# Vision-transformer front end with routed experts on one core: the image held on 96 partitions, its channel sums in two products, and the second norm in a tile of its own

## The reference, cut to what matters

```python
pooled = x.reshape(64, 12, 14, 16, 14, 16).sum(axis=(3, 5))   # image: sums over 16x16 patches
h = einsum('bcij,ce->bije', pooled, channel_weights)          # 196 tokens of 192 channels
h = concatenate([h.reshape(64, 196, 192), txt], axis=1)       # + 32 text tokens = 228
h = h + attention(layernorm(h))      # 12 heads of 16, causal, a sink per head, rotary q and k
xf = layernorm(h)                    # second norm: router logits, and the rows for the experts
h = h + experts(xf)                  # top 2 of 8, capacity, 192 -> 512 gated -> 192
```

## Time and profile before

| | before |
|---|---|
| median of three runs | 2927.87 us |
| the profiled execution's own time | 2924.14 us |
| its span, first to last instruction | 2922.3 us |
| PE busy | 2783.5 us (95%) |
| DVE busy | 2029.5 us (69%) |
| ACT busy | 1692.1 us (58%) |
| POOL busy | 2019.7 us (69%) |
| mean granted PE clock | 0.979 |
| moved by DMA | 292.47 MB |

### The profile page before, as it was taken

How to read it: one execution, slowest core, us unless ns; L and a number is a source line. 1 busy time by engine, 2 the same in 40 slices (tenths; PEclk the granted TensorE clock), 3 DMA queues, 4 the chain that set the end, 5 groups by cost and what they waited for, 6 DMA issues and landing times. The chain is left out here.

```text
span 2922.3 us, 65980 instructions
## 1 busy us (share of the span) xinstructions
PE 2783.5 (95%) x21712; PEld 2512.5 (86%) x21712; DVE 2029.5 (69%) x5657; ACT 1692.1 (58%) x4074; POOL 2019.7 (69%) x2070
## 2 busy tenths in 40 slices
PE   2899999999999999999999977999999999999998
PEld 1788888888888888888888866999999989999997
DVE  3577777777777777777777745767676767676766
ACT  0466666666666666666666644656565656565655
POOL 3578888888888888888888743656565655565665
PEclk8899999999999999999999978999999999999999
DMA  6455544444444444444344223333333333323242
GB/s 187 146 178 176 172 166 170 156 122 123 120 112 108 111 122 122 123 120 115 107 109 121 57 50 64 52 61 51 64 55 63 50 65 50 66 46 66 46 69 43
DMA packets 206006, 292.47 MB, mean 100 GB/s; under 512 B 95670, under 2 KB 167675, under 8 KB 205874
## 3 DMA queue, kind: packets, MB, share of 16 engines
q1 hardware_dynamic: 82642, 241.41, 28.1%
q0 software_dynamic: 122880, 47.00, 11.5%
q10 hardware_dynamic: 352, 2.41, 0.3%
HBM read 201.73 MB, written 93.90 MB: 101 GB/s over the span
## 5 line engine op out<-in xcount | busy, mean ns | idle before, releaser
L1494 POOL DMA_INDIRECT out<-arena,who x320 | 595.3, 1860 | 290.6 <-DVE who L1373 179.4
L572 DVE TENSOR_REDUCE top<-bank 114x2 f32<-114x456 f32 (+1 forms) x576 | 352.7, 622 | 85.9 <-PE bank L931 69.5
L687 POOL TENSOR_TENSOR arena<-arena 112x896 f32<-112x896 f32 x192 | 403.2, 2101 | 12.7 <-DMA arena<-in_x 12.7
L1467 PE MATMUL bank<-w_dn,hid 128*114 128x192 f32 x3840 | 401.9, 264 | 0.0
L1467 PEld LDWEIGHTS bank<-w_dn,hid 128*114 128x114 f32 x3840 | 390.3, 180 | 0.0
L1440 ACT ACTIVATE arena<-bank 128x456 f32<-128x456 f32 x320 | 176.2, 551 | 340.9 <-PE bank L1431 330.9
L1285 POOL DMA_INDIRECT moe_rows<-row,slot x256 | 293.8, 1148 | 102.8 <-issue 84.2
L549 ACT ACTIVATE pieces<-bank 64x456 fp32r<-64x456 f32 x384 | 209.2, 545 | 134.2 <-PE bank L907 131.9
L727 POOL TENSOR_TENSOR qk<-rot_c,qk 114x384 fp32r<-114x384 f32 x256 | 253.9, 1015 | 18.6 <-ACT qk L748 18.6
L1444 DVE TENSOR_TENSOR arena<-bank,arena 128x456 f32<-128x456 f32 x320 | 201.4, 630 | 93.7 <-ACT arena L1440 81.4
L1427 PE MATMUL bank<-pieces 128*128 128x456 f32 x640 | 240.1, 375 | 22.0 <-DVE arena L1444 15.4
(11 more groups left out here) (171 smaller groups left out, 7193.3 us busy)
## 6 DMA issues: line engine op xcount, KB each, us to landing
arena<-in_x SPq DMA_DIRECT2D x63, 2352.0 KB, 11.7
arena<-moe_rows SPq DMA_DIRECT2D x82, 363.4 KB
moe_rows<-filler SPq DMA_DIRECT2D x20, 1453.5 KB
out<-h SPq DMA_DIRECT2D x64, 171.0 KB
out<-arena,who POOLq DMA_INDIRECT x320, 5.0
arena<-in_w_t SPq DMA_DIRECT2D x9, 512.0 KB
arena<-in_w_t SPq DMA_DIRECT2D x18, 256.0 KB
moe_rows<-row,slot POOLq DMA_INDIRECT x256, 7.2
```

Source lines behind the costliest of these rows:

```text
L572: nc.vector.tensor_reduce(dst, src, AX.X, ALU.max).then_inc(maxed[k], 1)
L687: nc.gpsimd.tensor_tensor(xin[at.par][:, g, 0:mid], xin[at.par][:, g, 0:mid], xin[at.par][:, g, mid:XF], ALU.add).then_inc(x_folded, 1)
L1467: ins = nc.tensor.matmul(dst, hid2[:, j, h_part, at], w_dn2[e_par][:, j, w_part, :], start=(j == 0 and s % 2 == 0 and part == 0), stop=(j ...
L1494: nc.gpsimd.indirect_dma_start(out=out[:, :], out_offset=bass.IndirectOffsetOnAxis(ap=who[par][:, s:s + 1], axis=0), in_=ys[par][:, s, :], ...
```

## The change

Four edits, with what hangs on them:

1. The image lies on 96 partitions: 12 channels times 8 of the 16 rows of a patch, each partition holding for all 14 patch rows two image rows (1792 bytes in one run). It comes in 8 transfers of 12 partitions each. `fold_image` and `pool_image` now go over bands of patch rows (5, 5 and 4 bands of 224 values), and `pooled` holds 96 x 196 sums.
2. `spread_patches` and its table are gone. `sum_channels` multiplies `pooled` directly: one product for each token half.
3. The third `fold_image` of a step goes to the end of POOL's part, ahead of the scatter; the third `pool_image` goes behind `place_k` 1, ahead of `split_shift`.
4. `norm2_apply` writes to a tile `xf`; `turn_xf` reads it; a new ACT instruction `fill_row`, behind the last exponential of the step, copies it to `row[par]`. The wait for the scatter moves from `norm2_apply` to `fill_row` and to `assign`.

```diff
-GRP = 4
-NG = CH // GRP
-XP = GRP * SIDE * 2
-XF = HALF * IMG
+XP = CH * HALF
+XF = 2 * IMG
+BANDS = ((0, 5), (5, 10), (10, SIDE))
+NG = len(BANDS)
...
-            for g in range(NG):
-                sp.dma_start(chan[:, g, :], chan_w[GRP * g:GRP * (g + 1), :].unsqueeze(1)
-                             .to_broadcast([GRP, SIDE * 2, D])).then_inc(loaded, 16)
+            sp.dma_start(chan[:, :], chan_w.unsqueeze(0).to_broadcast([HALF, CH, D])).then_inc(loaded, 16)
...
-        x_img = x.rearrange("b (g c) (q r) w -> b (c q) g (r w)", g=NG, r=HALF)
+        x_img = x.rearrange("b c (i r s) w -> b r c i (s w)", r=HALF, s=2)
...
-            sp.dma_start(xin[at.par][:, :, :], x_img[at.b, :, :, :]).then_inc(x_loaded[at.par], 16)
+            for r in range(HALF):
+                sp.dma_start(xin[at.par][CH * r:CH * (r + 1), :, :], x_img[at.b, r, :, :, :]).then_inc(x_loaded[at.par], 16)
...
             if g == 0:
-                wait(dve, x_spread, at.b - 1)
+                wait(dve, h_summed, at.b - 1)
             dve.wait_ge(x_folded, NG * at.b + g + 1)
+            lo, hi = BANDS[g]
             ins = nc.vector.tensor_reduce(
-                pooled[at.par][:, g, :],
-                xin[at.par][:, g, 0:XF // 2].rearrange("p (r j c) -> p j r c", r=HALF // 2, c=PATCH), AX.XY, ALU.add)
+                pooled[at.par][:, SIDE * lo:SIDE * hi],
+                xin[at.par][:, lo:hi, 0:IMG].rearrange("p i (j c) -> p i j c", c=PATCH), AX.X, ALU.add)
...
+            wait(dve, scattered[at.par], 64 * at.half)     # in assign
...
-            pool.wait_ge(x_loaded[at.par], 16 * (at.half + 1))
-            mid = XF // 2
-            nc.gpsimd.tensor_tensor(xin[at.par][:, g, 0:mid], xin[at.par][:, g, 0:mid], xin[at.par][:, g, mid:XF],
+            pool.wait_ge(x_loaded[at.par], 16 * HALF * (at.half + 1))
+            lo, hi = BANDS[g]
+            nc.gpsimd.tensor_tensor(xin[at.par][:, lo:hi, 0:IMG], xin[at.par][:, lo:hi, 0:IMG], xin[at.par][:, lo:hi, IMG:XF],
                                     ALU.add).then_inc(x_folded, 1)
...
         def norm2_apply(act, at):
             act.wait_ge(ln2_step, 6 * (at.b + 1))
-            wait(act, scattered[at.par], 64 * at.half)
+            wait(act, xf_turned, at.b)
             for t in range(2):
-                ins = nc.scalar.activation(row[at.par][:, t, 0:D], h2[at.par][:, t, :], ACT.Identity,
+                ins = nc.scalar.activation(xf[:, t, :], h2[at.par][:, t, :], ACT.Identity,
...
+        def fill_row(act, at):
+            wait(act, scattered[at.par], 64 * at.half)
+            nc.scalar.activation(row[at.par][:, :, 0:D], xf[:, :, :], ACT.Copy).then_inc(row_filled, 1)
...
-            pe.wait_ge(x_spread, n)
+            pe.wait_ge(x_pooled, NG * n)
             wait(pe, v_ready, at.b)
             for t, (lo, hi) in enumerate(((0, TT), (TT, SIDE * SIDE))):
-                for g in range(NG):
-                    ins = nc.tensor.matmul(bank[6][0:hi - lo, D * t:D * (t + 1)], spread[:, g, lo:hi], chan[:, g, :],
-                                           start=(g == 0), stop=(g == NG - 1))
+                ins = nc.tensor.matmul(bank[6][0:hi - lo, D * t:D * (t + 1)], pooled[at.par][:, lo:hi], chan[:, :],
+                                       start=True, stop=True)
...
+            pool.wait_ge(row_filled, at.b + 1)     # in scatter_rows
```

More of the change, by code:

```diff
@@ L95 @@
 CONST_NAMES = ["cos", "sin", "ident", "mask_q0", "mask_k", "sel", "split", "small",
-               "before", "patch", "filler"]
+               "before", "filler"]
 class Batch:
@@ L166, in build @@
         ones = sb("ones", [TT, TT], bf16)
-        patch = sb("patch", [XP, SIDE])
         filler = sb("filler", [TT, 2, 2, RW], u32)
-        chan = sb("chan", [XP, NG, D])
+        chan = sb("chan", [XP, D])
         scale_col = sb("scale_col", [C, 2])
@@ L180, in build @@
         gate = sb("gate", [C, 2, E])
[L184 to L187, removed]
+        arena = sb("arena", [128, 2 * SIDE * XF])
+        xin = [arena[0:XP, SIDE * XF * i:SIDE * XF * (i + 1)].rearrange("p (i f) -> p i f", i=SIDE) for i in range(2)]
+        pooled = [sb(f"pooled{i}", [XP, SIDE * SIDE]) for i in range(2)]
         h = [sb(f"h{i}", [TT, 2, D]) for i in range(2)]
@@ L361, in setup_sync @@
                 (split[:, :], const["split"]), (small[:, :], const["small"]),
-                (patch[:, :], const["patch"]), (filler[:, :, :, :], const["filler"]),
+                (filler[:, :, :, :], const["filler"]),
                 (scale_col[:, :], norm_scale.rearrange("(c p) -> p c", p=C)),
@@ L683, in fold_image @@
         def fold_image(pool, at, g):
-            pool.wait_ge(x_loaded[at.par], 16 * (at.half + 1))
-            mid = XF // 2
-            nc.gpsimd.tensor_tensor(xin[at.par][:, g, 0:mid], xin[at.par][:, g, 0:mid], xin[at.par][:, g, mid:XF],
+            pool.wait_ge(x_loaded[at.par], 16 * HALF * (at.half + 1))
+            lo, hi = BANDS[g]
+            nc.gpsimd.tensor_tensor(xin[at.par][:, lo:hi, 0:IMG], xin[at.par][:, lo:hi, 0:IMG], xin[at.par][:, lo:hi, IMG:XF],
                                     ALU.add).then_inc(x_folded, 1)
-        def spread_patches(pool, at):
-            wait(pool, h_summed, at.b)
-            for g in range(NG):
-                pool.wait_ge(x_pooled, NG * at.b + g + 1)
-                ins = nc.gpsimd.tensor_tensor(spread[:, g, :].rearrange("p (i j) -> p i j", j=SIDE),
-                                              pooled[at.par][:, g, :].unsqueeze(1).to_broadcast([XP, SIDE, SIDE]),
-                                              patch[:, :].unsqueeze(2).to_broadcast([XP, SIDE, SIDE]), ALU.mult)
-            ins.then_inc(x_spread, 1)
         def inverse_std(pool, at, norm):
@@ L1021, in turn_xf @@
                 for t in range(2):
-                    ins = nc.tensor.transpose(bank[7][0:C, T * c + TT * t:T * c + TT * (t + 1)], row[at.par][:, t, C * c:C * (c + 1)],
+                    ins = nc.tensor.transpose(bank[7][0:C, T * c + TT * t:T * c + TT * (t + 1)], xf[:, t, C * c:C * (c + 1)],
                                               ident[0:TT, 0:TT])
@@ L1129, in step_scalar @@
             exps("7 8")
+            if z:
+                fill_row(act, z)
             if a:
@@ L1179, in step_vector @@
                 place_k(dve, a, 1)
+            if p:
+                pool_image(dve, p, 2)
             if m:
```

17 lines of the change are left out of this document (5 added, 12 removed).

## The result

The changed kernel takes **3261.9 us** (median, 3234.6 to 3279.5) where the kernel before took 2926.7 (2924.0 to 2928.7) beside it: a ratio of 1.114, 95% interval [1.1106, 1.1168]. The forecast was 2896, 1.1% faster. It is 11% slower. The profiled execution took 3234.6 us.

A forecast was written before the change was run, and what follows sets the result against it. PE was taken as the bound, with DVE's chain to `yn` a second bound half a microsecond below. Terms -31.7 - 4.7 + 3.6 + 1.0 = -31.8 us took 2924.1 to 2892.3; plus 3.7 gave 2896 us, range 2874 to 2916.

The forecast's parts named there:

- The image's transfers: Image loads: 12 engines instead of 16, 14.3 us an image instead of 10.7; hidden in steady state, 3.6 us at the start.
- The 20 filling steps: Steps with filler transfers: busiest DMA engines at 25.3 us in a 25.0 us step; 1 us for all, bounds 0 and 15.
- Start: Kernel start: text 0 lands behind image 1 and holds DVE, costing 3.6 us; first statistics at about 54 us.
- Later steps: Steady state: the slower image load is hidden in a window of some 30 us between issue and use.
- The ordinary step: Steps 3 to 63: shorter channel sums gain 0.52 us each, until PE waits for DVE's `yn`; 31.7 us in all.
- The third fold and patch sum: POOL's fold and DVE's sum ahead of `split_shift`: just on time, costed at nothing; bound 0.3 us a step.
- rival B: Third fold and patch sum push `split_shift` by about 0.3 us; step gain shrinks to 0.2 us, 2914 us; chance 15%.
- The second norm's tile: Second norm on ACT: own tile frees nothing now, but protects against a wait for the scatter; costed at nothing.
- Rival D: 12-row image transfers get as few engines as the filler: 27 us an image, 3250 us; 7% including milder forms.
- Rival A: PE stays the only bound and each step loses the whole 1.33 us: 2847 us; chance 5%.

The follow-up runs named there:

- e3: The kernel before the change with its image cut into 8 transfers of 14 adjacent partitions, 7168-byte runs kept: 3652.1 us, ratio 1.2501.
- e2: The changed kernel with each of the image's 8 transfers going to every eighth partition instead of 12 adjacent ones: 2970.8 us, ratio 1.0152.
- e11: The changed kernel, image still in 8 transfers of adjacent partitions, with only the filler's transfer split into 112 and 2 rows: 3173.0 us, ratio 1.0849.
- e1: The changed kernel with the image in one transfer over 96 partitions (other pixels summed, same work): 2930.0 us, ratio 1.0013.
- e7: e1 with the second norm as before the change, written into the row buffer after waiting for the scatter: 3081.3 us, ratio 1.0500.
- e16: e1 with e9's edit, the router's weights made one step later: 2844.4 us, ratio 0.9713.
- e18: e9 run again unchanged, in a later batch: 2853.9 us, ratio 0.9748, without delayed semaphores.
- e8: e2 with the filler's transfer sent as 112 and 2 rows, nothing else: 2934.4 us, ratio 1.0032.
- e9: e8 with the router's weights made one step later, behind the first norm's statistics: 3121.6 us, ratio 1.0655.
- e4: The kernel before the change with its one image transfer over 112 partitions in 1792-byte runs: 2928.0 us, ratio 1.0009.
- e5: e1 with the router's weights moved ahead of the last maxima, normalize moved earlier and their scratch in SBUF: 3301.8 us, ratio 1.1275.
- e13: e8 run again word for word on another chip: 3152.3 us, ratio 1.0760.

## Why the prediction was wrong

**The step that failed is "The image's transfers"**, and with it "The 20 filling steps". The prediction asked on how many engines a transfer runs and took the rate of an engine as given: 224 GB/s from an image over 112 partitions, times 12/16. The count was right (share 0.80 for 12 of 16, and 0.89 for e3's 14). By the Trainium skill (DMA: Bandwidth & Descriptors, "Why a DMA increments its semaphore by 16 and not by 1") a transfer gets the largest number of engines up to 16 that divides its outermost dimension, 12 and 14 here; the trace agrees. The rate was not right: 97 GB/s where 168 were reckoned. e2 shows that it would nearly have been with the partitions apart, 157 GB/s, 15.3 us for an image where 14.3 were reckoned. Adjacency, which the prediction did not look at, makes it 24.8.

- *Start.* Reckoned +3.6 us, for image 1. The text lands at 83.2, not at 54, 32.6 us later than before. Half of that, 16.1 us, is there at the first sum already: image 0 is slow too, which the prediction put at nothing without a word. The other half, for image 1, is in the first of the 21 steps (51.4 us where it was 34.9).
- *Filling steps.* Reckoned +1 us with a bound of 15. Measured +257 us for images 1 to 22. e11, with the filler over 112 partitions and the image as slow as in the change, has +58, its delayed semaphores included; so at least 199 of the 257 us are the filler on its few engines meeting the slow image on the same ones. The prediction had seen this meeting, "at the edge" at 25.3 us for the busiest engines; with 24.8 us for the image in place of 14.3 and 10.7 us for the filler an estimate is about 36, and the steps behind the first measure 32.5 to 41.4.
- *Later steps.* Reckoned hidden. DMA is busy 0.78 of the time, and the text comes late in some steps (DVE waits 52.5 us in 600 for it): 36 us in 42 steps.

**The ordinary step.** The 0.52 us were right where they were read: step 64 has no image, and the first steps of e1 take 24.98 us. They were wrong for most steps, by three things of which step 64 showed nothing. The CAST on the same DVE chain slid under POOL's scatter issue (+0.27 us); the prediction watched `split_shift`, which starts at T0 + 2.91 as forecast, and not the instructions behind it. PE's new wait at `turn_yn` (0.9 us, not 0.7) costs clock every sixth step. And the loop's end, no longer hidden, costs 0.17 us every second step. e1, without slow transfers, is thus at 1.0013 of before: the forecast's gain is gone with that alone.

**The third fold and patch sum** cost nothing, as forecast, and rival B did not happen: `split_shift` starts at T0 + 2.91 in e1. **The second norm's tile** was costed at nothing and said to protect; it protects by 150 us (e7), more than anything else in the change, and e3 shows what slow transfers cost without it.

**Rival D** was the nearest, 3250 for 3262, with 7%, by luck: six engines at full rate would have moved 89 GB/s, and twelve slowed ones moved 97. Its reason, as few engines as the filler, was wrong, and its shape too (41 x 2 and 20 x 12, against 36 and 257). **Rival A**'s 2847 is what the change gives once loads and DVE chain are mended: e16 has 2844, e18 2854, with no wait of PE for `yn` in either.

What stays open: why e8 and e9 take 2934 and 2854 on some chips and 3152 and 3115 on another (each batch had a chip of its own; the delay showed in the third and fourth). The delayed semaphores are shown; that SP's eight issues have a part in them is argued from their place in time, and from the kernel before, which issues one transfer and kept its time beside them. No form of the changed kernel with a single transfer (e1, e16) was run on such a chip, which would have tested it. The changed kernel itself was profiled once, without the delay; e11, with 1232.9 us for images 22 to 64 against 1108.5, says that it could cost it some 120 us more, an estimate.

## What to carry to other kernels

Price a transfer by two numbers, how many DMA engines it gets and what each moves, and take the second from a transfer of the same placement in SBUF. Here rows dealt out over the partitions moved 157 GB/s and rows packed side by side 97. Look also for two narrow transfers that are under way at once, since they can want the same engines. A gain that is read from one special step needs a look at every instruction on the chain that the shift of half a microsecond moves past another engine's. And if a set of edits all lose alike, run the unedited one again beside them before believing it.

## What the runs showed of the hardware that was not expected

- Eight transfers of 12 or 14 adjacent partitions move 97 and 104 GB/s with 0.80 and 0.89 of the DMA engines busy (after, e3); the same 12 rows spread over every eighth partition 157 GB/s with 0.80 (e2).
- Runs of 1792 bytes in place of 7168 over 112 partitions cost nothing (e4, 1.0009).
- Some DVE instructions with all operands in SBUF (a CAST, a TENSOR_SCALAR, a TENSOR_TENSOR) end only with POOL's running instruction, a scatter's issue, a product or a fold: 0.42 us for 0.16 (e1), 0.76 for 0.16 and 1.81 for 0.17 (e5). A RECIPROCAL beside the same fold was not held (e5).
- When a scatter lands depends on the loads beside it: 7.3 us after its issue before, 5.6 in e2, 11.4 in e1 and 19.0 in e3 (medians between 900 and 1500 us).
- With a wait of PE of 0.9 us in each step the granted clock was at its lower level in one step of six (e1), and never between 200 and 1600 us once the wait was gone (e18); with waits of 2 us it is 0.88 on the mean over the run (e5).
- One program, two times: 2934 (e8) and 3152 (e13), with TensorE's semaphore updates 1 to 3.3 us late in nearly each step of the slower. It repeats within 0.6% on its chip, while the kernel before beside it moved from 2927.8 to 2930.2.
